# A graph layer in split float32 on one core: the rounded and remainder rings with every bank's 500 columns on a multiple of 2,048 bytes

## What is computed

```python
# x, item_feat: 10000 x 128; adj: 10000 x 10000; W_item, W_user: 128 x 128
h_user = maximum(layernorm(x), 0.0)
h = item_feat @ W_item.T + b_item
b = h_user @ W_user.T + b_user
out = x + relu(adj @ h + b)
```

## Time and profile before

| what | value |
|---|---|
| runs of the kernel before | 1143.09 us median of 3 (1141.33 to 1143.35) |
| the profiled execution | 1141.89 us, its span 1140.3 us |
| mean granted TensorE clock | 0.999 of 2.4 GHz |
| TensorE matmul busy | 1119.8 us, 98% |
| TensorE weight loads busy | 923.5 us, 81% |
| VectorE busy | 975.2 us, 86% |
| ScalarE busy | 773.2 us, 68% |
| GpSimd busy | 20.3 us, 2% |
| moved by DMA | 416.38 MB, mean 365 GB/s |

### The profile page before, as it was taken

How to read it: one execution, slowest core, us unless ns; L and a number is a source line. 1 busy time by engine, 2 the same in 40 slices (tenths; PEclk the granted TensorE clock), 3 DMA queues, 4 the chain that set the end, 5 groups by cost and what they waited for, 6 DMA issues and landing times.

```text
span 1140.3 us, 14338 instructions
## 1 busy us (share of the span) xinstructions
PE 1119.8 (98%) x5078; PEld 923.5 (81%) x5078; DVE 975.2 (86%) x683; ACT 773.2 (68%) x502; POOL 20.3 (2%) x42
## 2 busy tenths in 40 slices
PE   6999999999999999999999999999999999999998
PEld 5888888878888888788888887888888878888886
DVE  5989988888898878898898888988888889888886
ACT  4766766667677676666677666767666767767663
POOL 0000000000000000000000000000000000000000
PEclk9999999999999999999999999999999999999999
DMA  9999999999999999999999999999999999999993
GB/s 358 397 407 365 351 367 371 353 360 354 388 370 363 363 384 381 374 374 374 357 370 370 374 390 361 384 363 373 360 380 369 386 360 387 371 370 354 356 394 123
DMA packets 62659, 416.38 MB, mean 365 GB/s; under 512 B 7644, under 2 KB 9124, under 8 KB 62608
## 3 DMA queue, kind: packets, MB, share of 16 engines
q1 hardware_dynamic: 59984, 406.38, 92.8%
q0 software_dynamic: 2624, 9.22, 2.4%
HBM read 410.45 MB, written 5.12 MB: 364 GB/s over the span
## 4 chain that ended last, share of the span: by engine, by line
PE 97%; issue 1%; ACT 1%; DMA 1%; DVE 1%; SPq 0%; DVEq 0%; ACTq 0%
PE acc L508 31%; PE acc L515 31%; PE acc L510 31%; PE spare L464 2%; PE acc L497 1%; PE spare L484 1%; PE spare L490 1%; ACT hi_ring L277 1%; DMA items<-in_item_t 1%; DVE y L397 0%; DVE lo_ring L340 0%; PE acc L525 0%; DVEq L94 0%; SPq L199 0%; SPq L188 0%
## 5 line engine op out<-in xcount | busy, mean ns | idle before, releaser
L340 DVE TENSOR_TENSOR lo_ring<-a_ring,hi_ring 128x2000 fp32r<-128x2000 f32 x390 | 870.3, 2241 | 140.7 <-ACT hi_ring L277 140.2
L277 ACT CAST hi_ring<-a_ring 128x2000 fp32r<-128x2000 f32 x390 | 728.9, 1869 | 347.5 <-PE acc L515 344.0
L508 PE MATMUL acc<-hi_ring,h_lo 128*128 128x500 f32 x1560 | 619.7, 397 | 4.5 <-DVE y L397 4.5
L515 PE MATMUL acc<-lo_ring,h_hi 128*128 128x500 f32 x1560 | 606.4, 389 | 0.0
L510 PE MATMUL acc<-hi_ring,h_hi 128*128 128x500 f32 x1560 | 604.6, 388 | 0.0
L508 PEld LDWEIGHTS acc<-hi_ring,h_lo 128*128 128x128 f32 x1560 | 293.4, 188 | 68.1 <-DVE y L397 7.8
L510 PEld LDWEIGHTS acc<-hi_ring,h_hi 128*128 128x128 f32 x1560 | 293.6, 188 | 61.2 <-issue 4.6
L515 PEld LDWEIGHTS acc<-lo_ring,h_hi 128*128 128x128 f32 x1560 | 293.4, 188 | 60.0
L464 PE MATMUL spare<-wi,items 128*128 128x128 f32 x156 | 23.9, 294 | 10.8 <-DMA items<-in_item_t 9.0
L464 PEld LDWEIGHTS spare<-wi,items 128*128 128x128 f32 x156 | 23.0, 206 | 13.0 <-issue 7.1
L345 DVE TENSOR_TENSOR h_full<-spare,bi 128x384 f32<-128x384 f32 x26 | 14.3, 552 | 10.6 <-PE spare L464 10.6
(11 more groups left out here) (29 smaller groups left out, 113.9 us busy)
## 6 DMA issues: line engine op xcount, KB each, us to landing
a_ring<-in_adj_tiles SPq DMA_DIRECT2D x390, 1000.0 KB, 6.9
rows<-in_x_rows POOLq DMA_DIRECT2D x20, 250.0 KB, 7.6
items<-in_item_t SPq DMA_DIRECT2D x12, 384.0 KB, 6.9
out_t<-y POOLq DMA_DIRECT2D x16, 250.0 KB, 5.4
out_t<-y SPq DMA_DIRECT2D x4, 250.0 KB, 2.2
a_rem<-in_adj_rem SPq DMA_DIRECT2D x20, 31.2 KB, 4.2
items<-in_item_t SPq DMA_DIRECT2D x2, 192.0 KB, 5.2
wi<-in_w_item_t SPq DMA_DIRECT2D x1, 64.0 KB, 1.8
```

Source lines behind the costliest of these rows:

```text
L277: nc.scalar.copy(hi_ring[:, r, :], a_ring[:, s, 0:GROUP_W]).then_inc(hi_written, 1)
L340: nc.vector.tensor_tensor(lo_ring[:, r, :], a_ring[:, s, 0:GROUP_W], hi_ring[:, r, :], ALU.subtract).then_inc(lo_written[s], 1)
L508: nc.tensor.matmul(acc[k][:, 0:BANK_W], h_lo[:, c, :], hi_ring[:, r, cols], start=(c == 0), stop=False, skip_group_check=True)
L515: last = nc.tensor.matmul(acc[k][:, 0:BANK_W], h_hi[:, c, :], lo_ring[:, r, cols], start=False, stop=False, skip_group_check=True)
```

## The change

The order of the declarations is another, with an unused tensor `gap` of 96 columns, and both split rings have a fourth dimension: [slots, 4 banks, 512 columns], of which 500 are used. The rings now begin at byte 18,432 (hi) and 43,008 (lo), both multiples of 2,048, and as a bank takes 2,048 bytes, every bank of every slot does. `h_hi` begins at 67,584, `h_lo` at 107,520, `a_ring` at 147,456. The slots of `a_ring` are 8,000 bytes apart, with nothing between them. ScalarE and VectorE write their 2,000 columns as four runs of 500; what they read from `a_ring` is one run of 2,000 as before, and VectorE's second source has the four runs too. The tiles in HBM keep their pitch of 2,048 columns. The instructions on each engine are the same in number and order.

```diff
@@ constants
+BANK_PITCH = 512
+RING_GAP = 96
@@ graph_layer
-        a_ring = sb("a_ring", [P, A_SLOTS, PITCH])
-        hi_ring = sb("hi_ring", [P, S_SLOTS, GROUP_W], F32R)
-        lo_ring = sb("lo_ring", [P, S_SLOTS, GROUP_W], F32R)
-        h_hi = sb("h_hi", [P, CHUNKS, HID], F32R)
-        h_lo = sb("h_lo", [P, CHUNKS, HID], F32R)
-
-        a_rem = sb("a_rem", [P, BANK_W])
-        h_rem = sb("h_rem", [P, HID])
         wi = sb("wi", [P, HID])
         wu = sb("wu", [P, HID])
         bi = sb("bi", [P, HID])
+        sb("gap", [P, RING_GAP])
+
+        hi_ring = sb("hi_ring", [P, S_SLOTS, ACC_BANKS, BANK_PITCH], F32R)
+        lo_ring = sb("lo_ring", [P, S_SLOTS, ACC_BANKS, BANK_PITCH], F32R)
+        h_hi = sb("h_hi", [P, CHUNKS, HID], F32R)
+        h_lo = sb("h_lo", [P, CHUNKS, HID], F32R)
+        a_ring = sb("a_ring", [P, A_SLOTS, GROUP_W])
+
+        a_rem = sb("a_rem", [P, BANK_W])
+        h_rem = sb("h_rem", [P, HID])
@@ load_tile
-                sp.dma_start(a_ring[:, s, 0:GROUP_W], adj_tiles[bass.ds(tile, 1), :, 0:GROUP_W].rearrange("o p n -> (o p) n")).then_inc(a_loaded[s], 16)
+                sp.dma_start(a_ring[:, s, :], adj_tiles[bass.ds(tile, 1), :, 0:GROUP_W].rearrange("o p n -> (o p) n")).then_inc(a_loaded[s], 16)
@@ round_hi
-                nc.scalar.copy(hi_ring[:, r, :], a_ring[:, s, 0:GROUP_W]).then_inc(hi_written, 1)
+                nc.scalar.copy(hi_ring[:, r, :, 0:BANK_W], a_ring[:, s, :].rearrange("p (k n) -> p k n", n=BANK_W)).then_inc(hi_written, 1)
@@ subtract_lo
-                nc.vector.tensor_tensor(lo_ring[:, r, :], a_ring[:, s, 0:GROUP_W], hi_ring[:, r, :], ALU.subtract).then_inc(lo_written[s], 1)
+                nc.vector.tensor_tensor(lo_ring[:, r, :, 0:BANK_W], a_ring[:, s, :].rearrange("p (k n) -> p k n", n=BANK_W),
+                                        hi_ring[:, r, :, 0:BANK_W], ALU.subtract).then_inc(lo_written[s], 1)
@@ group (TensorE)
-                        cols = slice(k * BANK_W, (k + 1) * BANK_W)
-                        nc.tensor.matmul(acc[k][:, 0:BANK_W], h_lo[:, c, :], hi_ring[:, r, cols],
+                        nc.tensor.matmul(acc[k][:, 0:BANK_W], h_lo[:, c, :], hi_ring[:, r, k, 0:BANK_W],
-                        nc.tensor.matmul(acc[k][:, 0:BANK_W], h_hi[:, c, :], hi_ring[:, r, cols],
+                        nc.tensor.matmul(acc[k][:, 0:BANK_W], h_hi[:, c, :], hi_ring[:, r, k, 0:BANK_W],
-                        last = nc.tensor.matmul(acc[k][:, 0:BANK_W], h_hi[:, c, :], lo_ring[:, r, cols],
+                        last = nc.tensor.matmul(acc[k][:, 0:BANK_W], h_hi[:, c, :], lo_ring[:, r, k, 0:BANK_W],
```

## The result

The changed kernel takes 1138.65 us (median of 8 runs, 1136.76 to 1139.94) against 1142.47 us (8 runs, 1141.14 to 1143.35) of the kernel before in the same session: a ratio of 0.9967, 95% interval 0.9958 to 0.9976. It is faster, by 3.8 us; the forecast was 17.8. The profiled execution took 1139.03 us.

The account below looks back on a forecast made before the run. The prediction took TensorE's big matmuls, 0.2258 us start to start, as the bound. 17.8 us less from the moving operands, all else nothing, took 1141.89 to 1124.1; 1.2 more for the median gave 1125.3 us, range 1,105 to 1,156.

Parts of the forecast that it names:

- Part 1: TensorE's big matmuls: aligned column starts cut each gap from 0.2258 to 0.222 us, 17.8 us less over 4,680.
- its own signs of being wrong: Gaps still differing between slots, a common gap of 0.226 or more, or a subtraction longer than about 2.6 us.
- Parts 2 to 4: ScalarE's rounding and VectorE's subtraction in four runs, and the dense raw ring's loads: each costed at nothing.
- Part 5: Weights: both arrays started and still start at multiples of 512 bytes, costed at nothing.
- Rival (a): Matmul gaps lose their whole excess, falling to 0.208 to 0.215 us: 1,061 to 1,092 us; chance 0.12 including what lies between.
- Rival (b): The start of a matmul's column run plays no part, mean gap stays: 1,141 to 1,145 us; chance 0.16.
- Rival (c): Columns and weights all on multiples of 512 is a bad alignment, gaps up to 0.230: 1,153 to 1,163 us; chance 0.22.

Follow-up runs that it names:

- e3: Changed kernel with all banks of both rings starting 16 bytes past a multiple of 2,048, weights still on 512: 1138.52 us, ratio 0.9966 to the kernel before.
- e6: Changed kernel with both weight arrays 64 bytes later, moving columns still on 2,048: 1119.77 us, one run.
- e7: Changed kernel with both weight arrays 256 bytes later: 1140.54 us, one run.
- e11: Changed kernel with rings and weights all 64 bytes later, so their distance stays: 1140.28 us, one run.
- e10: Changed kernel with weights 128 bytes past a multiple of 512: 1145.51 us, one run.
- e1: Changed kernel with the banks 2,000 bytes apart again, new declaration order and dense raw ring kept: 1144.06 us, ratio 1.0011 to the kernel before.
- e2: Changed kernel with banks 2,112 bytes apart, each on a multiple of 64 bytes: 1147.69 us, ratio 1.0048 to the kernel before.
- e12: Changed kernel with weights 64 bytes later, timed again in five runs: 1119.03 us, ratio 0.9792 to the kernel before.
- e5: Changed kernel with the three big matmuls taking 448 of each bank's 500 columns: 1056.71 us, one run.

## Why the prediction was wrong

**Part 1, the moving operands**, is the step that failed. It took the gaps of two pairs of 0.44 us, at 0 and 32 bytes past a multiple of 256, for what such a start gives by itself, and put every gap at 0.222, 0.0038 us less. It measured 0.0010 less, on average. The pairs were read nearly right (0.444 and 0.448 us by the start times in full, 0.222 and 0.224 a gap), but they were moments of a mixture of 24 starts, in which a gap also depends on the ones before it. The same start, on its own, gives 0.2233 or 0.2267 (after), and a start 16 bytes past gives the same (e3). What the gap follows is the distance of the weights' start from the columns' start, modulo 256 bytes (e6, e7, e11, e3; modulo 128 is ruled out by e10). The rows of the kernel before could not tell the two apart: its weights lie on multiples of 512, so that a start's place in a block of 256 bytes and its distance from the weights are one number. At the distance of 0 that this change happens to choose, the gain is small.

The time of 1138.65 us lies in the forecast's own range, 1,118 to 1,140 us, and so does the mean gap. That is luck: it is the mean of two rhythms that the forecast did not have, and of its own signs of being wrong the dear rhythm, 0.2267, meets one (a gap of 0.226 or more).

**Parts 2 to 4** held. The copies kept their durations, the breaks cost VectorE nothing, TensorE never waited for a subtraction, and the loads stayed covered, also in the kernel of 1,119 us, where ScalarE waits 3.4 us for them. **Part 5** costed the weights at nothing since they stay on multiples of 512. That was true of their place; that they were the other half of the matter, the sum had no term for.

**Rival (a)** did not come: no kernel here has a gap near 0.211 at 500 columns. The 211 ns that the Trainium skill gives (TensorE: Matmul & The Clock Gate, section Back-to-back issue gap) are not reached; it calls them the gap of matmuls by themselves, and here each matmul has a weight load of its own. The best rhythm is 220.0, the worst 228.9. **Rival (b)**, no effect, lies outside the interval by 0.2%, and e1 to e3 show that the starts play a part. **Rival (c)** looked in the right place and had the wrong sign: a conflict within TensorE's own reads, weights against columns. What spoke against it, a cheap run near a multiple of 512, was no evidence, being one moment of the mixture; and it was priced at the distance of 0 only. The dear distances are 32, 128 and in one phase 0 and 192. Asked as "which distance is good?", it would have led to e6.

That the reads of weights and columns of one engine get in each other's way is an explanation that all these runs fit, but it is argued and not shown; what stands shown is that the gap follows their distance and a phase that side work changes. The Trainium skill (SBUF — State Buffer, section SBUF: two separate sides) says that on the engines' side only the port pair of VectorE and GpSimd causes contention, and that TensorE waits for nobody. If the explanation is right, the last does not hold for TensorE against itself: moving the weights against the columns (what else moves is excluded by e11) gives 0.2200 in place of 0.2249, a ratio of 0.9792 in place of 0.9967.

**Open.** Why 64 is the good distance and 192 has two extremes, and what a piece of side work does to the phase, was not found; the mean gaps fit whole blocks of 8 columns at six distances (66, 67 and 68 of them, 0.0033 us each), but at 32 and 192 averages of 0.2280 and 0.2289 occur that are no whole number. The period of 256 rests on e7. The remaining multiples of 16 bytes, and a different distance for `h_hi` and `h_lo`, were not tried with equal starts.

## What to carry to other kernels

Where one engine streams two operands from SBUF, read the timeline start to start, and look for gaps that repeat exactly by slot and bank: they are a hint that addresses play in. Give all moving operands equal starts (2,048 bytes apart here), so that the distance to the weights is the same for each matmul, and then try that distance: here the pitch alone gave 0.3%, and with the weights 64 bytes on it gave 2.1%. A pattern of short gaps at some addresses does not tell what those addresses would give by themselves.

## What was not expected of the hardware

Padding can hurt: banks 2,112 bytes apart, each on a multiple of 64 bytes (e2), are 0.3% slower than banks packed at 2,000 in the same layout (e1) and 0.5% slower than the kernel before. And with the faster matmuls, one of the group boundaries sees TensorE's clock fall, after it had waited 1.2 us for VectorE to empty a bank. In the kernel of e12, two windows at the third group's start (engines' busy times, then PEclk, DMA share, GB/s):

```profile
462.00:465.60 3.60, 2.41 (x15) 1.13 (x14) 3.60 (x4) 1.86 (x1) 0.21 (x1) 1.00 1.01 407
465.60:469.00 3.40, 3.40 (x10) 2.72 (x9) 2.99 (x3) 0.00 (x0) 1.98 (x4) 0.51 0.99 338
```

Before the fall, TensorE was busy for 2.41 of 3.60 us. At the granted clock of 0.51, the 1.2 GHz level, gaps are 0.41 to 0.42 us, that is 500 columns at 1.2 GHz (0.4167) and next to nothing beside them: the excess is gone at half clock. The first gaps of the product last 0.415 to 0.419 us too, at the mixed distances of the kernel before and at the distance of 0 alike, though the record of the clock reads 1.00 there. The stretch costs some 1.6 us. It lay at another boundary in e6 (the fourth group's), 448 columns (e5) have it at two, and neither the kernel before nor the changed one has it at any. The wait alone does not bring it: each of the four boundaries has one of 1.1 to 1.2 us, in the kernel before too.
